# A third buffer for gathered rows, six-block loops and a reordered index load in the edge-message pass of a graph-network kernel

## The reference, cut to what matters

```python
msg_in   = concatenate([nodes[row], nodes[col], edge_features], axis=-1)   # 64 + 64 + 32
messages = relu(msg_in @ mW1 + mb1) @ mW2 + mb2
aggregated = segment_sum(messages, col, num_segments=12500)
```

## Time and profile before

| | us |
|---|---|
| median of three runs | 13430.48 (13422.02 to 13433.54) |
| profiled execution, first to last instruction (span) | 13426.1 |
| line 1316 for the first time in `wide` | 8245.6 |
| line 1316 for the last time | 13308.2 |
| POOL busy, line 1289 | 3041.0 |

### The profile page before, as it was taken

How to read it: one execution, slowest core, us unless ns; L and a number is a source line. 1 busy time by engine, 2 the same in 40 slices (tenths; PEclk the granted TensorE clock), 3 DMA queues, 4 the chain that set the end, 5 groups by cost and what they waited for, 6 DMA issues and landing times. The chain is left out here.

```text
span 13426.1 us, 144231 instructions
## 1 busy us (share of the span) xinstructions
PE 7285.8 (54%) x52956; PEld 5571.9 (42%) x52956; DVE 6792.6 (51%) x8156; ACT 2832.8 (21%) x2654; POOL 6380.1 (48%) x6717
## 2 busy tenths in 40 slices
PE   9755545555555455589999994333333333333334
PEld 4333333333333333379989994222222222222223
DVE  5566666666666666632232224444444444444445
ACT  4333333333333333320000001111111111111112
POOL 4456565656565656400000004555555665555564
PEclk9877777677767666689999997666666666666667
DMA  9732323232323233379979994333333333333332
GB/s 388 290 107 97 106 97 106 98 106 98 106 97 106 97 105 99 106 267 370 370 292 370 371 370 116 87 88 88 88 86 85 87 88 88 87 88 87 85 86 66
DMA packets 480426, 2020.11 MB, mean 150 GB/s; under 512 B 193465, under 2 KB 246136, under 8 KB 354776
## 3 DMA queue, kind: packets, MB, share of 16 engines
q1 hardware_dynamic: 205304, 1283.59, 27.3%
q0 software_dynamic: 206272, 317.25, 10.1%
q10 hardware_dynamic: 68768, 418.23, 8.6%
HBM read 1385.92 MB, written 632.61 MB: 150 GB/s over the span
## 5 line engine op out<-in xcount | busy, mean ns | idle before, releaser
L1289 POOL DMA_INDIRECT big<-Pd,mt x3223 | 3041.0, 944 | 2127.8 <-DMA mt<-in_meta 1186.2
L428 POOL DMA_INDIRECT big<-Yd,ix x3223 | 3041.5, 944 | 2069.5 <-PE ps L535 1095.7
L462 DVE TENSOR_TENSOR ring<-ps,vw 128x2940 bf16<-128x2940 f32 (+1 forms) x516 | 1725.9, 3345 | 1761.8 <-PE ps L529 1516.3
L527 PE MATMUL ps<-ring 128*128 128x490 bf16 x3223 | 1427.4, 538 | 1999.5 <-DVE ring L465 1190.3
L1316 DVE TENSOR_TENSOR ps<-ps,big 128x1024 f32<-128x1024 f32 x403 | 494.9, 1229 | 2656.3 <-remote 2397.2
L527 PEld LDWEIGHTS ps<-ring 128*128 128x128 bf16 x3223 | 416.3, 129 | 2802.4 <-issue 1835.0
L1423 PE MATMUL ps<-idt,total 128*128 128x128 f32 x135 | 63.8, 473 | 2716.1 <-DVE total L1329 2716.1
L535 PE MATMUL ps<-big 128*65 128x128 f32 x6446 | 1149.9, 346 | 555.3 <-issue 554.6
L535 PEld LDWEIGHTS ps<-big 128*65 128x65 f32 x6446 | 1045.9, 185 | 651.7 <-issue 644.9
L1423 PEld LDWEIGHTS ps<-idt,total 128*128 128x128 f32 x135 | 24.4, 181 | 2814.7 <-DVE total L1329 2814.7
L549 ACT ACTIVATE Z<-ps 128x1470 bf16<-128x1470 f32 (+1 forms) x584 | 800.1, 1399 | 1790.2 <-PE ps L529 755.2
(11 more groups left out here) (215 smaller groups left out, 11561.0 us busy)
## 6 DMA issues: line engine op xcount, KB each, us to landing
Yd<-big SPq DMA_DIRECT2D x196, 1024.0 KB, 8.8
Aj<-Z SPq DMA_DIRECT2D x65, 3062.5 KB
big<-Aj SPq DMA_DIRECT2D x130, 1531.2 KB, 8.3
cb<-Aj ACTq DMA_DIRECT2D x130, 1531.2 KB, 8.5
Aj<-big SPq DMA_DIRECT2D x64, 3062.5 KB
cb<-Aj SPq DMA_DIRECT2D x128, 1531.2 KB, 8.4
Z<-Aj ACTq DMA_DIRECT2D x128, 1531.2 KB, 8.5
dr<-in_dstr SPq DMA_DIRECT2D x135, 1152.0 KB
```

The source lines that it names most:

```text
L428: e.indirect_dma_start(gv[j][:, k, 0:64], None, table, bass.IndirectOffsetOnAxis(ap=ix[j][:, k:k + 1], axis=0)).then_inc(sm[f"g{j}"], 16)
L462: nc.vector.tensor_tensor(one[r][:, 0:m, :], bc_t(iof, m, W * NT), bc_f(vw[j][:, k], m, W * NT), ALU.is_equal)
L527: nc.tensor.matmul(PS[q][:, 0:W * NT], olo[r][:, c, :], one[r][:, c, :], start=True, stop=False)
L1289: e.indirect_dma_start(gv[j][:, k, :], None, Pd, bass.IndirectOffsetOnAxis(ap=mt[j][:, k:k + 1], axis=0)).then_inc(sm[f"g{j}"], 16)
```

## The change

A third buffer `rows[2]` for gathered rows is added; block b uses `rows[b % 3]`, with three semaphores g0, g1, g2 in place of two. POOL, VectorE and SP loop over six blocks (`six_blocks`), since 2 and 3 buffers come together only every sixth block; TensorE and ScalarE keep the loop of two. `x2` starts at 2, so POOL's block b waits for the third part of block b - 3. SP's turn is split: the index load of block b + 2 now waits for the landed gathers of block b (and for `rel`, VectorE's use of the table), and only `dr` and the edge features wait for the third part of block b. `prep` gets a wait on its own earlier result (`ot`).

```diff
+        def six_blocks(e, turn, count):
+            turn(0, 0, 0, 0, 0)
+            with e.Fori(0, (count - 3) // 6, 1) as i:
+                for u in range(1, 7):
+                    turn(6 * i + u, u % 2, 3 * i + u // 2, u % 3, 2 * i + u // 3)
+            for b in (count - 2, count - 1):
+                turn(b, b % 2, b // 2, b % 3, b // 3)
...
-            gv = [G[j][:, 0:K * P].rearrange("p (k n) -> p k n", n=P) for j in range(2)]
+            rows = [G[0][:, 0:K * P], G[1][:, 0:K * P], s.enter_context(nc.sbuf_tensor("rows2", [P, K * P], F32))[:, :]]
+            gv = [v.rearrange("p (k n) -> p k n", n=P) for v in rows]
...
             def sync(e):
+                def indices(b, j):
+                    e.dma_start(mt[j][:, 0:MW], meta[b]).then_inc(sm[f"m{j}"], 16)
+
                 def load(b, j):
-                    e.dma_start(mt[j][:, 0:MW], meta[b]).then_inc(sm[f"m{j}"], 16)
                     e.dma_start(dr[:, :], dstr[b].to_broadcast([HR, K * P])).then_inc(sm["dq"], 16)
                     e.dma_start(te[j][HR:P, :], efT[b].rearrange("f c n -> f (c n)")).then_inc(sm[f"f{j}"], 16)
 
-                def turn(b, j, i):
+                def turn(b, j, i, m, h):
                     if type(b) is not int or b + 2 < NB:
-                        e.wait_ge(sm["x2"], reg(e, b + 2))
+                        e.wait_ge(sm[f"g{m}"], 16 * K * h + 16 * K)
+                        e.wait_ge(sm["rel"], reg(e, b + 1))
+                        indices(b + 2, j)
+                        e.wait_ge(sm["x2"], reg(e, b + 3))
                         load(b + 2, j)
...
             def gpsimd(e):
-                def turn(b, j, i):
+                def turn(b, j, i, m, h):
...
-                        e.indirect_dma_start(gv[j][:, k, :], None, Pd,
+                        e.indirect_dma_start(gv[m][:, k, :], None, Pd,
...
-                short_blocks(e, turn, NB)
+                six_blocks(e, turn, NB)
...
             def vector(e):
-                e.sem_inc(sm["x2"], 1)
+                e.sem_inc(sm["x2"], 2)
...
                 def prep(j, loaded, n, row):
                     e.wait_ge(sm[f"m{j}"], loaded)
+                    if type(n) is not int or n > 1:
+                        e.wait_ge(sm["ot"], n - 1)
...
-                    high(2, reg(e, b + 2))
+                    high(2, reg(e, b + 3))
```

More of the change, by code:

```diff
@@ L1261, in sync @@
                         e.dma_start(qw[j][h][HR:P, :], mW1[128:160, :]).then_inc(sm["w"], 16)
+                def indices(b, j):
+                    e.dma_start(mt[j][:, 0:MW], meta[b]).then_inc(sm[f"m{j}"], 16)
                 def load(b, j):
-                    e.dma_start(mt[j][:, 0:MW], meta[b]).then_inc(sm[f"m{j}"], 16)
                     e.dma_start(dr[:, :], dstr[b].to_broadcast([HR, K * P])).then_inc(sm["dq"], 16)
                     e.dma_start(te[j][HR:P, :], efT[b].rearrange("f c n -> f (c n)")).then_inc(sm[f"f{j}"], 16)
-                def turn(b, j, i):
+                def turn(b, j, i, m, h):
                     if type(b) is not int or b + 2 < NB:
-                        e.wait_ge(sm["x2"], reg(e, b + 2))
+                        e.wait_ge(sm[f"g{m}"], 16 * K * h + 16 * K)
+                        e.wait_ge(sm["rel"], reg(e, b + 1))
+                        indices(b + 2, j)
+                        e.wait_ge(sm["x2"], reg(e, b + 3))
                         load(b + 2, j)
+                indices(0, 0)
                 load(0, 0)
+                indices(1, 1)
                 e.wait_ge(sm["ot"], 1)
                 load(1, 1)
-                short_blocks(e, turn, NB)
+                six_blocks(e, turn, NB)
                 for j in range(2):
@@ L1288, in turn @@
                     for k in range(KL if at(b, NB - 1) else K):
-                        e.indirect_dma_start(gv[j][:, k, :], None, Pd,
+                        e.indirect_dma_start(gv[m][:, k, :], None, Pd,
                                              bass.IndirectOffsetOnAxis(ap=mt[j][:, k:k + 1], axis=0)
-                                             ).then_inc(sm[f"g{j}"], 16)
-                short_blocks(e, turn, NB)
+                                             ).then_inc(sm[f"g{m}"], 16)
+                six_blocks(e, turn, NB)
             def vector(e):
-                e.sem_inc(sm["x2"], 1)
+                e.sem_inc(sm["x2"], 2)
                 nc.vector.tensor_copy(ioP, io[:, :]).then_inc(sm["io"], 1)
@@ L1312, in targets, with gather @@
                                             ALU.is_equal).then_inc(sm["oh"], 1)
-                def gather(q, j, n):
+                def gather(q, m, n):
                     e.wait_ge(sm[f"p{q}"], n)
-                    nc.vector.tensor_tensor(step[q], step[q], G[j][:, SW * q:SW * (q + 1)], ALU.add).then_inc(sm[f"x{q}"], 1)
+                    nc.vector.tensor_tensor(step[q], step[q], rows[m][:, SW * q:SW * (q + 1)], ALU.add).then_inc(sm[f"x{q}"], 1)
                 def middle(q, n):
@@ L1342, in turn @@
                         prep(1 - j, 16 * (i + 1 + j), reg(e, b + 2), 16 * b + 32)
-                    e.wait_ge(sm[f"g{j}"], 16 * K * i + 16 * (KL if last else K))
-                    gather(0, j, n)
+                    e.wait_ge(sm[f"g{m}"], 16 * K * h + 16 * (KL if last else K))
+                    gather(0, m, n)
                     if last:
@@ L1350, in turn @@
                         return
-                    gather(1, j, n)
+                    gather(1, m, n)
                     middle(0, n)
-                    gather(2, j, n)
+                    gather(2, m, n)
                     if not first:
@@ L1620, in build @@
         edge_phase(["m0", "m1", "f0", "f1", "dq", "w", "io", "ot", "oh", "rel", "pool", "ag", "tr", "sm", "acc"] + [
-            f"{n}{q}" for n in ("p", "x", "hi", "y", "c", "o") for q in range(3)], wide, "g0", "g1", "si")
+            f"{n}{q}" for n in ("p", "x", "hi", "y", "c", "o") for q in range(3)], wide, "g0", "g1", "g2", "si")
         phase(["w", "o", "p1", "p2", "p3", "p4", "c1", "c2", "c3", "c4", "cp", "d", "v", "r", "ld", "lq",
```

## The result

| | before | after |
|---|---|---|
| median of the runs, us | 13432.01 (13422.02 to 13436.12, 4 runs) | 13804.83 (13788.91 to 13808.64, 4 runs) |
| profiled execution, span, us | 13426.1 | 13805.1 |
| ratio | 1 | 1.0275, interval 1.026 to 1.0289 |

The change makes the kernel 2.75% slower; 13785 us was predicted. The experiments ran on four chips: on three of them (5, 9 and 4) the kernel before takes 11280 to 11291 us, on the fourth (14) 13428 us as here, so a time is compared only with that of the kernel before on the same chip.

What follows compares the result with a forecast made beforehand. It took POOL's gathers, TensorE's recovery while POOL pauses and POOL's restart to bound the kernel: 8350 + 130 x 40.5 + 19 + 146.5 = 13780 us, median 13785 us, range of 8 in 10 from 13300 to 14330.

Steps and rivals of the forecast that it cites:

- The restart: In `wide`, third add to POOL's first gather takes 10.8 us against 3.96, the index table held behind 1536 KB.
- POOL's gathers and the recovery: In `wide`, POOL gathers two blocks in 59.3 us, then TensorE recovers in about 10 us.
- the case that the prediction named as close to its number: In `wide`, POOL runs two blocks for each pause: 10.8 + 59.3 + 10 = 80.1 us, 40.1 each.
- rival 2: In `wide`, the third part never comes while POOL gathers: 44.7 us a block, 14330 us; chance 0.17.
- rival 4: In `wide`, the longer pause makes it faster: below 37.8 us a block, at 35 the time is 13070; chance 0.18.
- The start: Start of `wide`: POOL first stops at 8334, third add of block 1 comes at 8350 instead of 8318.69, 31 us lost.
- The end: End of `wide`: block 132 takes some 19 us, then 146.5 us from its third add to the span's end.
- The sum: Whole span: 8350 + 130 x 40.5 + 19 + 146.5 = 13780 us; median 13785 us, 2.6% slower.
- The terms at nothing: In `wide`, loops of six, the wait on `ot`, and the wait on landed gathers and `rel` cost 0.
- lower bound: In `wide`, third add to third add takes at least 29.5 us, with 17.5 for TensorE's last 48 instructions.
- sign of a pause of 4 to 15 us: In the profile after, POOL pauses 4 to 15 us once a block, or once in two blocks with 48 gathers.
- rival 3: In `wide`, signals come in time, POOL never waits and gathers alone bound it: about 12400 us; chance 0.05.

Runs made afterwards that it cites:

- g2: Changed kernel with the third add of block b waiting for the landed rows of block b + 2; 12958.69 us, 1.1487 times the kernel before.
- g4: Kernel e1 with the third add of block b waiting for the landed rows of block b + 2; 11755.05 us, 1.042 times the kernel before.
- g6: Kernel g2 with small `dr` and feature loads, 144 KB ahead of the index load instead of 1536 KB; 13809.43 us, 1.0281 times the kernel before.
- e3: Changed kernel with the index load right behind the wait for `x2`, ahead of `dr`, without its two earlier waits; 11292.96 us, 1.0002 times the kernel before.
- f1: Changed kernel, unedited, run again beside the kernel before; 11280.42 us, ratio 1.0001.
- e1: Changed kernel with the index load of block b + 3 issued before SP's wait for the third add of block b; 11305.5 us, ratio 1.0013.
- h2: Changed kernel with the third add of block b waiting until POOL has issued all gathers of block b + 2; 11298.09 us, ratio 1.0016.
- h4: Kernel e1 with the third add waiting for POOL's issue of its gathers, as in h2; 11298.22 us, 1.0016 times the kernel before.
- e2: Kernel before, two buffers kept, with the index load issued ahead of the wait for the third add; 11291.27 us, ratio 1.0.
- e4: Kernel before with line 1408 reading fp32 operands' upper halves as bf16, 98 TensorE instructions a block instead of 146; 11291.37 us, ratio 1.0.
- g1: Kernel before with the third add of block b waiting for the landed rows of block b + 1; 11988.16 us, ratio 1.0626.
- h1: Kernel before with the third add of block b waiting until POOL has issued all gathers of block b + 1; 11279.46 us, ratio 1.0.

## Why the prediction was right

**The restart.** 10.8 us predicted, 11.20 measured in the median, and 11.22 in g2 in a condition with punctual signals. It was put together from an estimate of 6.6 to 7.5 us for 1536 KB, 0.5 for the table and 0.85 for release. g4 differs from g2 only in where SP issues the table, and its restart is 9.1 us shorter, more than the 7.3 us that the change adds; g6 shows that bytes make the larger part of these. e3 with the same wait, the table issued first and the third buffer kept, would be the closest test and was not run.

**POOL's gathers and the recovery.** 59.3 us for 48 gathers against 59.7 measured (the 0.3 us between two blocks was left out), and 10 against 10.0 to 10.1. This is the case that the prediction named as close to its number: two blocks for each pause, 80.1 us predicted, 80.92 measured. The 10 us of recovery were a value picked between 4.2 and 14.7, not worked out; that it was met is in part luck. The third adds inside a cycle (17.92 and 63.0 us apart) show that one pause of POOL lets TensorE through two blocks, which decides against rival 2 (44.7 us a block) and rival 4 (a short pause in each block).

**The start.** The third add of block 1 was put at 8350 and came at 8373.32. Of these 23.3 us, 23.0 are there before `wide` gathers anything (first gather at 8237.37, before at 8214.40). They are no effect of the change in `wide`: in the typed pass, which the diff doesn't touch, POOL's gathers are busy 3049.0 us instead of 3041.5 and idle 2086.1 instead of 2069.5, 24.1 us together. From the first gather of `wide` to the end of the span the change costs 5567.7 - 5211.7 = 356.0 of the 379.0 us between the two spans. POOL then ran 96 gathers to 8357.16, 119.8 us after its first, as predicted (8334 - 8214.4 = 119.6); the recovery was 16.2 us, where 15 to 16 were taken.

**The end.** 19 us predicted for block 132, 17.92 measured; 146.5 from there to the end, measured 13805.1 - 13658.89 = 146.2.

**The sum.** 8373.3 + 130 x 40.52 + 17.9 + 146.2 = 13805.0, against 13780. The missing 25 us are nearly all the late start of `wide`. That 40.5 meets 40.52 is partly luck: the worked case gave 40.1, and 0.4 us were added only because 40.5 was near the middle of a range held likely. The terms of that case came out 0.8 us too low for two blocks, which filled the gap.

**The terms at nothing.** Loops of six, third buffer and the wait on `ot`: f1 and e3 show at most 0.1% for all of them, where POOL never pauses. The page of after has 38 instruction loads where before had 36. e1, h2 and h4 are 14 to 18 us slower than the kernels beside them, and most of it stands at the tail: from the end of the last gather to the last run of the add are 19.6 us in e1 and 22.9 in h2 and h4, against 7.1 in f1. With these edits the adds run later behind the gathers, which costs nothing until the gathers end.

**What was not right.** Inside the cycle the prediction's lower bound for the time from one third add to the next was 29.5 us (17.5 us for TensorE's last 48 instructions, after 12); the next add came after 17.92. The 17.5 us were taken from before, where the second add is late behind matmuls that have run. In after all three sets of 16 matmuls are through at 8470.26, 5.0 us after POOL's restart, and the add follows 1.9 us later. What it concluded from the bound, that a time under 29.8 us lets POOL run two blocks, held all the more. Its sign of a pause of 4 to 15 us missed as well: the pause is 21.27 us, as its own 10.8 + 10 would have given.

The prediction used TensorE's late signals as if they were a property of this kernel, and gave "signals come in time and POOL never waits" 0.05 as rival 3. On three of the four chips that followed this is just what happens: 30.0 us a block in f1, e2, e3 and e4, the same time for the kernel before and after, and the change costs nothing. The 2.75% hold where signals are late. Rival 3 was judged by the trace of one measurement, which can't show how far its own condition reaches. Two figures beside the sum are slightly off and change nothing in it: 3223 gathers at 0.94 + 0.30 us from 8214 end at 12210, not 12240, and 38 us a block gives 13460, not 13480.

**Open.** Why TensorE's signals come late in one condition isn't settled. The traces taken there hold 53,000 to 56,000 semaphore updates, all others 144,000 to 146,000, so the releasers that they name ("remote", "issue", the index load) are less sure than those of g1, g2 and g4; whether updates were missing in the record or merged on the chip they don't say. No run changed the order of loads and nothing else where signals come late, so there the 7.3 us of the longer restart rest on g1, g2 and g4, and on g6 for the bytes. That an early index load (e1) would gain there is not shown: from g4's restart and the earlier trace rows, 29.65 + 4.23 + 2.04 = 35.9 us a block would give about 13200 us, an estimate that no run has tested.

## What to carry to other kernels

A load that is moved earlier in the text of a stream is early only if nothing in front of it in that stream waits for the event it should precede. Trace one block's small load to its place between the waits and the bulk loads of its queue, and put small urgent tables ahead of bulk ones: here that place was worth 7 us in each pause. A buffer more does not remove a wait as long as another input of the producer comes with the same event: here POOL's idle time in the pass rose from 2127.8 to 2465.0 us.

## What the runs showed of the hardware

- One unchanged kernel takes 11280 to 11291 us (medians) on three chips, and 13428 us on a fourth and 13432 in the first measurement. The difference (2148 us) lies in POOL's pauses in the two passes that gather: over the same 96 gathers TensorE gets through 115 matmuls in 120 us in the one condition and 266 in the other. Measure a change in a gather-bound pass on more than one chip.
- POOL's instruction stream ran 12 gathers (14.0 us) ahead of the engine in h1, so a semaphore that POOL raises behind a DMA says that the instruction has been passed on, not that it has been worked off.
- Small loads in SP's queue move behind the bulk loads issued before them: from its issue to POOL's start the 48.5 KB table needed 2.53 us when issued first (medians of before and g1), 4.69 behind 144 KB (g6) and 8.7 behind 1536 KB (g2 and after). The Trainium skill (DMA: Bandwidth & Descriptors, Queues, rings and completion order) has each DMA engine take SP's descriptors in the order of its ring; g2 agrees, where the table's 160 packets follow the 1.57 MB of the loads ahead.
